# State space scan: in seven units of the last chunk GpSimd multiplies the states with C instead of VectorE

## The reference

```python
proj = jnp.einsum('blh,oh->bol', x, W_in); h, gate = jnp.split(proj, 2, axis=1)
h = silu(causal_depthwise_conv(h, conv_w) + conv_b)           # I = 512 channels, 4 taps
ts, Bm, Cm = jnp.split(jnp.einsum('bil,oi->blo', h, Wx), [R, R + N], axis=-1)   # R = 128, N = 16
ts, Bm, Cm = rms(ts), rms(Bm), rms(Cm)
delta = softplus(jnp.einsum('blr,ir->bil', ts, Wdt) + dt_bias)
def step(s, inp):                                             # s: [batch, I, N], over 256 steps
    s = jnp.exp(d_t[..., None] * A) * s + d_t[..., None] * B_t[:, None, :] * u_t[..., None]
    y = jnp.einsum('bin,bn->bi', s, C_t)
y = (ys + D * h) * silu(gate);  out = y @ Wout.T
```

## Time and profile before

| | us |
|---|---|
| median of 3 runs | 1913.19 (1912.94 to 1915.3) |
| the profiled execution's own time | 1918.9 |
| its span, first to last instruction | 1917.0 |
| TensorE busy in the span | 1812.9 (95%) |
| VectorE busy | 1339.2 (70%) |
| ScalarE busy | 943.0 (49%) |
| GpSimd busy | 576.9 (30%) |

### The profile page before, as it was taken

The page is one execution under the profiler, slowest core; times in us unless marked ns, Lnnn a source line. Parts: engine busy times, 40 slices in busy tenths (PEclk is TensorE's granted clock), DMA queues, the critical chain, the costliest instruction groups (busy, mean ns, idle before and its releaser), DMA issues.

```text
span 1917.0 us, 26237 instructions
## 1 busy us (share of the span) xinstructions
PE 1812.9 (95%) x9417; PEld 1378.8 (72%) x9417; DVE 1339.2 (70%) x1876; ACT 943.0 (49%) x1778; POOL 576.9 (30%) x397
## 2 busy tenths in 40 slices
PE   7999999999799999987789999999999999999998
PEld 5888888887354544433357888888888887777887
DVE  6666656567999999999975666565675555666533
ACT  4442333333688687684434433233333338888422
POOL 1000234000488878888710000000000025555000
PEclk9999999999899999999999999999999998999999
DMA  5232345120222222223102323231121306553100
GB/s 195 84 97 72 97 146 135 61 63 21 67 72 72 70 68 77 72 72 112 61 17 51 91 96 106 61 108 61 61 77 46 64 1 137 109 108 74 38 12 23
DMA packets 84187, 146.40 MB, mean 76 GB/s; under 512 B 13849, under 2 KB 23705, under 8 KB 83545
## 3 DMA queue, kind: packets, MB, share of 16 engines
q1 hardware_dynamic: 84056, 144.72, 26.5%
HBM read 130.38 MB, written 14.29 MB: 75 GB/s over the span
## 4 chain that ended last, share of the span: by engine, by line
PE 70%; DVE 16%; issue 6%; ACT 6%; DMA 1%; POOL 0%; DVEq 0%; SPq 0%; ACTq 0%; POOLq 0%
PE psum L161 19%; PE psum L162 18%; PE psum L163 18%; DVE scan_state L1608 8%; PE psum L1434 4%; PE psum L1982 2%; PE psum L1358 1%; PE psum L1329 1%; ACT psum L1542 1%; DVE moe_hidden_lo L850 1%; DVE scan_state L1615 1%; ACT L1485 1%; DVE X L807 1%; PE psum L1961 1%; ACT attn_p L2124 1%
## 5 line engine op out<-in xcount | busy, mean ns | idle before, releaser
L1207 POOL TENSOR_TENSOR scan_state<-scan_delta_u,scan_B_rows 128x1024 f32<-128x1024 f32 x127 | 299.5, 2367 | 99.9 <-PE psum L1434 85.7
L161 PE MATMUL psum<-xnT_hi,moe_w_hi 128*128 128x512 f32 x800 | 316.8, 396 | 6.3 <-DVE xnT_lo L470 6.3
L162 PE MATMUL psum<-xnT_lo,moe_w_hi 128*128 128x512 f32 x800 | 314.8, 393 | 0.0
L163 PE MATMUL psum<-xnT_hi,moe_w_lo 128*128 128x512 f32 x800 | 312.6, 391 | 0.0
L778 ACT ACTIVATE moe_hidden<-psum 128x512 f32<-128x512 f32 x200 | 119.6, 598 | 385.4 <-PE psum L163 385.3
L1608 DVE TENSOR_TENSOR_SCAN scan_state<-psum,scan_state 128x1024 f32<-128x1024 f32 x128 | 292.0, 2282 | 0.5 <-ACT psum L1542 0.4
L827 DVE TENSOR_TENSOR moe_gated_up<-moe_gate_rows,psum 128x512 f32<-128x512 f32 x184 | 126.4, 687 | 210.9 <-PE psum L163 121.3
L1434 PE MATMUL psum<-scan_state,ident 128*128 128x512 f32 x512 | 246.7, 605 | 4.6 <-DVE scan_gated L1623 3.4
L418 POOL TENSOR_SCALAR rstd<-mean_var 128x2 f32<-128x2 f32 x48 | 10.6, 220 | 763.5 <-DVE mean_var L452 763.1
L161 PE MATMUL psum<-moe_w_hi,moe_hidden_hi 128*128 128x256 f32 x800 | 230.3, 288 | 4.7 <-DVE moe_hidden_lo L850 3.6
L1542 ACT ACTIVATE psum<-scan_delta,scan_A 128x510 f32<-128x510 f32 x256 | 165.7, 679 | 126.8 <-DVE scan_state L1608 124.3
(11 more groups left out here) (225 smaller groups left out, 3479.7 us busy)
## 6 DMA issues: line engine op xcount, KB each, us to landing
scan_B_rows<-scan_B SPq DMA_DIRECT2D x127, 256.0 KB, 3.1
moe_gate_rows<-gate_table SPq DMA_DIRECT2D x176, 128.0 KB, 3.0
moe_w_raw<-moe_pack SPq DMA_DIRECT2D x50, 384.0 KB, 3.9
attn_stack<-attn_rows SPq DMA_DIRECT2D x96, 128.0 KB, 5.2
moe_gate_rows<-gate_table SPq DMA_DIRECT2D x32, 224.0 KB, 3.1
ffn_w_raw<-ffn_pack SPq DMA_DIRECT2D x16, 384.0 KB, 4.0
moe_gate_rows<-gate_table SPq DMA_DIRECT2D x32, 160.0 KB, 2.7
moe_gate_rows<-gate_table SPq DMA_DIRECT2D x24, 192.0 KB, 2.9
```

What stands on the lines that cost most here:

```text
L161: e.matmul(out, wH, xH, start=start, stop=False)
L162: e.matmul(out, wH, xL, start=False, stop=False)
L163: return e.matmul(out, wL, xH, start=False, stop=stop)
L1207: e.tensor_tensor(self.st[q % self.NBUF][:], self.dtu[:, 2 * h:2 * h + 2, :], self.Bs[:, q % self.RING, :].unsqueeze(1).broadcast_to([P, 2 ...
```

## The change

Seven units of the last chunk (`POOLED`: 2, 13, 17, 20, 23, 26, 29 within the chunk) are handled in another way. VectorE skips their product with C and TensorE skips the spread of their C row. SyncE instead spreads the C row with a DMA into a new buffer `Cs` in SBUF (one buffer, so each waits for the GpSimd product before it); this DMA is issued ahead of the B row of unit q+2. The table in HBM therefore holds 32 rows (B and C) and not 16, in all chunks. GpSimd multiplies the state buffer with that row, in its step q behind `inputs(q+3)`. TensorE takes the sum of such a unit one step later: in step q+1, after the wait for VectorE's product of unit q+1 and the spread, it waits for GpSimd's product and adds unit q, then unit q+1. The counts of the semaphores `z` and `C` are taken over the units that VectorE multiplies (`weighed`).

```diff
@@ -1018,6 +1018,7 @@
     NBUF = 4
     LAST = {12: ("ln0", 1 - NCH), 18: ("ln1", 1 - NCH)}
     RING = 4
+    POOLED = (2, 13, 17, 20, 23, 26, 29)
     BOTH = "natural_log_exp_and_others"
     BANK = 7
     ENDS = (7, 4)
@@ -1048,6 +1049,7 @@
         self.s_delta, self.s_dtu, self.s_Du = Sem(k, "delta"), Sem(k, "dtu"), Sem(k, "Du")
         self.s_dA, self.s_m, self.s_scan = Sem(k, "dA"), Sem(k, "m"), Sem(k, "scan")
         self.s_C, self.s_z, self.s_y, self.s_yg = Sem(k, "C"), Sem(k, "z"), Sem(k, "y"), Sem(k, "yg")
+        self.s_crow, self.s_zp = Sem(k, "crow"), Sem(k, "zp")
         self.s_o, self.s_tap, self.s_b0 = Sem(k, "o"), Sem(k, "tap"), Sem(k, "b0")
         tail.by_act, tail.s_pw = 2, Sem(k, "pw", 4, passes=NCH)
 
@@ -1086,6 +1088,7 @@
         self.mean = [new("mean_ts", [P, P]), new("mean_bc", [2 * NST, 2 * NST])]
         self.eps = new("eps", [P, 1])
         self.dtb, self.A, self.D = new("dt_bias", [P, IB]), new("A", [P, IB, NST]), new("D", [P, IB])
+        self.Cs = new("C_row", [P, CHUNK])
         self.eye, self.pick = new("state_pick_raw", [P, 2 * NST]), new("state_pick", [P, 2 * NST], F32R)
         assert a.off <= k.nc.sbuf_usable_end, a.off
         acc = Arena(k, tag)
@@ -1108,6 +1111,17 @@
 
         c, r = divmod(q, 2 * NST)
         return c, r // NST, r % NST
+
+    def pooled(self, q):
+
+
+        c, r = divmod(q, self.UNITS)
+        return c == NCH - 1 and r in self.POOLED
+
+    def weighed(self, q):
+
+        n = sum(self.pooled(x) for x in range(q + 1))
+        return q + 1 - n, n
 
     def job(self, q):
 
@@ -1147,15 +1161,25 @@
                           (self.mean[1], "mean_bc")):
             e.dma_start(dst[:], i[name]).then_inc(self.s_load.sem, 16)
 
+    def c_row(self, e, q):
+
+        used = self.weighed(q)[1] - 1
+        if used:
+            e.wait_ge(self.s_zp.sem, self.s_zp.at(used))
+        c, h, n = self.unit(q)
+        e.dma_start(self.Cs[:], self.table[c, NST + n].partition_broadcast(P)).then_inc(self.s_crow.sem, 16)
+
     def sync(self, e):
         for q in range(self.N):
             c, h, n = self.unit(q)
+            if q >= 2 and self.pooled(q - 2):
+                self.c_row(e, q - 2)
             if q == self.N - self.UNITS + 12 and self.next:
                 self.emptied(e)
                 self.next.first(e)
             if q % self.UNITS == 0:
                 e.wait_ge(self.s_nm.sem, self.s_nm.at(2 * c + 2))
-                e.dma_start(self.table[c], self.wt[1][0:NST, :]).then_inc(self.s_kept.sem, 16)
+                e.dma_start(self.table[c], self.wt[1][:]).then_inc(self.s_kept.sem, 16)
                 e.wait_ge(self.s_kept.sem, self.s_kept.at(16 * (c + 1)))
             if q > self.RING:
                 e.wait_ge(self.s_m.sem, self.s_m.at(q - self.RING + 1))
@@ -1208,6 +1232,13 @@
                             self.Bs[:, q % self.RING, :].unsqueeze(1).broadcast_to([P, 2, CHUNK]),
                             ALU.mult).then_inc(self.s_m.sem, 1)
 
+        def weigh(q):
+            st, n = self.st[q % self.NBUF], self.weighed(q)[1]
+            e.wait_ge(self.s_scan.sem, self.s_scan.at(q + 1))
+            e.wait_ge(self.s_crow.sem, self.s_crow.at(16 * n))
+            e.tensor_tensor(st[:], st[:], self.Cs[:].unsqueeze(1).broadcast_to([P, 2, CHUNK]),
+                            ALU.mult).then_inc(self.s_zp.sem, 1)
+
         for slot in (0, 2):
             self.before.pool(e, NCH - 1, slot)
         for q in range(1, 3):
@@ -1220,6 +1251,8 @@
                 self.normed(e, c + 1, 1)
             if q + 3 < self.N:
                 inputs(q + 3)
+            if self.pooled(q):
+                weigh(q)
             if r in (6, 8, 9, 11):
                 (self.lose, self.lost, self.step, self.times_u)[(6, 8, 9, 11).index(r)](e, c, 1)
             if r in (24, 25, 26, 28) and c + 1 < NCH:
@@ -1411,6 +1444,8 @@
             e.wait_ge(self.s_relu.sem, self.s_relu.at(2))
 
         def spread(q):
+            if self.pooled(q):
+                return
             c, h, n = self.unit(q)
             if q and q % self.UNITS == 0:
                 e.wait_ge(self.s_bc.sem, self.s_bc.at(c + 1))
@@ -1418,21 +1453,29 @@
             e.matmul(ps[:, 6, :], self.pick[:, x:x + 1].broadcast_to([P, P]), self.bc[:, c % 2, :], start=True,
                      stop=True).then_inc(self.s_C.sem, 1)
 
+        def total(q):
+            n = q % NST
+            for m in range(2):
+                x = e.matmul(ps[:, 4 + m, :], k.ident[:], self.st[q % self.NBUF][:, m, :], start=(n == 0), stop=(n == NST - 1))
+            x.then_inc(self.s_y.sem, 1)
+
         begin()
         spread(0)
         for q in range(self.N):
             c, h, n = self.unit(q)
             if n == 0 and q:
-                e.wait_ge(self.s_z.sem, self.s_z.at(q + 1))
+                e.wait_ge(self.s_z.sem, self.s_z.at(self.weighed(q)[0]))
                 spread(q + 1)
                 e.wait_ge(self.s_yg.sem, self.s_yg.at(2 * c + h))
             if n or not q:
-                e.wait_ge(self.s_z.sem, self.s_z.at(q + 1))
+                e.wait_ge(self.s_z.sem, self.s_z.at(self.weighed(q)[0]))
                 if q + 1 < self.N:
                     spread(q + 1)
-            for m in range(2):
-                x = e.matmul(ps[:, 4 + m, :], k.ident[:], self.st[q % self.NBUF][:, m, :], start=(n == 0), stop=(n == NST - 1))
-            x.then_inc(self.s_y.sem, 1)
+            if q and self.pooled(q - 1):
+                e.wait_ge(self.s_zp.sem, self.s_zp.at(self.weighed(q)[1]))
+                total(q - 1)
+            if not self.pooled(q):
+                total(q)
             if self.job(q):
                 job(self.job(q), self.BANK)
             for m in self.DIAG.get(q % self.UNITS, ()):
@@ -1609,9 +1652,11 @@
                                  ALU.add).then_inc(self.s_scan.sem, 1)
 
         def weigh(q):
+            if self.pooled(q):
+                return
             st = self.st[q % self.NBUF]
             e.wait_ge(self.s_scan.sem, self.s_scan.at(q + 1))
-            e.wait_ge(self.s_C.sem, self.s_C.at(q + 1))
+            e.wait_ge(self.s_C.sem, self.s_C.at(self.weighed(q)[0]))
             e.tensor_tensor(st[:], st[:], ps[:, 6, :].unsqueeze(1).broadcast_to([P, 2, CHUNK]), ALU.mult).then_inc(self.s_z.sem, 1)
 
         def gate(c, h):
@@ -2405,7 +2450,7 @@
         tails = [Tail(k, "t0_", entry=True, route=True)]
         pack = nc.dram_tensor("ffn_pack", [FFN_TILES, P, Glu.WCOLS], F32, kind="Internal").ap()
         gates = nc.dram_tensor("gate_table", [NEXP, TOK], F32, kind="Internal").ap()
-        states = nc.dram_tensor("scan_B", [NCH, NST, CHUNK], F32, kind="Internal").ap()
+        states = nc.dram_tensor("scan_rows", [NCH, 2 * NST, CHUNK], F32, kind="Internal").ap()
         rows = nc.dram_tensor("attn_rows", [2, 2, NCH, HID, CHUNK], F32, kind="Internal").ap()
         fixed = nc.dram_tensor("attn_fixed", [2, 64, CHUNK], F32, kind="Internal").ap()
         parts = []
```

## The result

The change made the kernel slower: 1925.37 us median of 4 runs (1922.42 to 1928.03) against 1914.14 (1912.94 to 1915.3), ratio 1.0056 [1.0043, 1.0068]. Five more runs gave 1926.96 against 1914.39, ratio 1.006 [1.0048, 1.0072]. The forecast was 1915.9 in a range up to 1920.5: the side was right, the size was not.

The account below looks back on a forecast made before the run. VectorE was taken to bound the last chunk before the change, GpSimd's loop after it. 2.4 us saved and 5.1 us lost to TensorE's half clock gave +2.7, so 1915.9 us, range 1908.5 to 1920.5.

Parts of the forecast that it names:

- The bound and the gross saving: VectorE sets the last chunk's pace; seven multiplies leaving it save 1.27 us each, 8.9 us in all.
- Unit 2: At TensorE's output job: it starts 1.71 us earlier and scan 5 moves from 872.30 to 870.6, saving 1.7 us.
- Unit 13: GpSimd's multiply comes only after input 16 ends at 907.3; of 3.0 us saved so far, 1.5 is left.
- The loop: Units 17 to 29: GpSimd's multiply, wait for TensorE's sum and three inputs take 11.4 us; 2.4 us saved overall.
- TensorE's clock: Bursts of sums after TensorE's waits: three of five run at half clock, 1.71 us each, costing 5.1 us.
- every burst slow: Rival: TensorE's bursts all at half clock; five give +6.2 us, 1919.4, six give 1921.1; chance 0.18.
- The sum again: The forecast's total for the change: -2.4 + 5.1 = +2.7 us.
- the step that carried the change over: Profiled execution 1918.9 becomes 1921.6; the shown median, 1913.19, is 5.7 below it, so the forecast is 1915.9 us.
- Rows by DMA, table, skipped spreads: Seven C rows, the 32-row table and seven spreads left out on TensorE: taken as 0 us.
- The row of unit 22: B row queued behind C row 20 after multiply 17: lands at 928.9, wanted at 929.4, hidden by 0.5 us.

Follow-up runs that it names:

- e3: The change, with matmuls that add 0 to the open sums filling TensorE's waits: 1916.01 us, 1.0015 to the kernel before.
- e10: The change's program with the 32-row table and no units given to GpSimd: ratio 1.0001 to the kernel before.
- e4: The change, with GpSimd's multiply of unit q put ahead of the input of unit q+3: 1915.08 us, 1.0001 to the kernel before.
- e11: The change with only units 2, 17, 21, 25, 29 given to GpSimd, order as in the change: ratio 1.0037 to the kernel before.
- e12: The change with only units 17, 20, 23, 26 given to GpSimd: 1920.6 us, 1.0034 to the kernel before.
- e1: Only the change's 32-row table and seven C row DMAs, which nobody reads; VectorE and TensorE do all units: ratio 1.0009 to the kernel before.
- e9: The change itself run again, nothing altered: 1926.96 us, 1.006 to the kernel before.
- e8: The change's program with no units given to GpSimd and matmuls adding 0 behind units 5, 12, 21, 23, 26, 28: 1.0015 to the kernel before.
- e2: The change with only unit 2 given to GpSimd: ratio 0.9998 to the kernel before.
- e6: The change with only units 2 and 26 given to GpSimd: ratio 0.9987 to the kernel before.

## Why the prediction was wrong

- **The bound and the gross saving** were right. VectorE's multiplies left, and two scans in a row take 4.46 (2.19 forecast from start to start).
- **Unit 2**: 1.5 us gained up to scan 5 (1.7 forecast). Right.
- **Unit 13**: GpSimd's multiply at 906.85, 56.1 after scan 0; forecast 907.3, that is 56.0 after it. Right, but the burst behind it was already slow: scan 17 lies 67.4 after scan 0, where 65.2 was forecast and before had 66.7.
- **The loop**: right in kind and in length (11.4 forecast, 11.5 in e3). Its result, 2.4 us saved, was too good: e3 shows 0 against before's stretch with one slow burst of 1.0 us, so some 1 us saved, and against e10's stretch a loss of 1.4. The sum had started from the execution with both long weight splits (2.23 and 3.02) and called them part of the loop; where one is short anyway (e10) there is 2.1 less to save. The order experiment (e4) shows that it was a matter of order and not of GpSimd's load.
- **TensorE's clock**: this step failed, by its size. The prediction took 3 of 5 bursts from the share among five waits of before, 5.1 us. Six of six were slow. GpSimd's waits are 1.85 longer four times and 1.0 once, and the last burst 1.7: 10.1 us. The granted clock's level and the price of a slow sum were right; the share was wrong. It was counted over the length of waits, and length alone does not tell: the last burst was slow behind 1.49 and 0.93 us, and behind the same wait for the gate of unit 16 a sum was slow in e11 (first line) and not in e12 (second):

```profile
918.63 3.21 PE L1459 MATMUL psum<-scan_state,ident 128*128 128x512 f32 x4 [2.47 <-DVE scan_gated L1668]
917.77 1.96 PE L1459 MATMUL psum<-scan_state,ident 128*128 128x512 f32 x4 [2.46 <-DVE scan_gated L1668]
```

  That waits close together are what made all six slow is my reading and not shown. The rival "every burst slow" (six: 1921.1) was the nearest. The Trainium skill (TensorE: Matmul & The Clock Gate, Part 1: The HAM clock gate) has the array slow until activity releases it. This trace agrees for the four bursts that began at the low level, and not for the two that began at full clock and fell 1 us in.
- **The sum again**: with these terms -1 + 10.1 = +9 for the stretch, against 8.7 measured from before's; +1.4 + 10.1 = +11.5 against 11.0 measured from e10's. The first, carried to the median, is 1923, 2 to 4 us short of the runs; the second is 1925.6, and the runs gave 1925.4 and 1927.0. So the step that carried the change over from an execution 5.7 us above the median hid some 2 us.
- **Rows by DMA, table, skipped spreads**: 0 was right (e1, e10). The row of unit 22, forecast as hidden by 0.5 us, released no wait: all of GpSimd's waits from 905 on end with TensorE's sums.
- **What was in it only once**: TensorE's in-order wait holds back the C rows for VectorE (2.95 at unit 16; 6.2 in e11). For unit 16 the prediction had 1.0.

## What to carry to other kernels

Work given to an idle engine pays only if its result is wanted late: here the spare 41 us did not help, because each product stood behind an input that nobody needed yet and in front of one that waited for it; with the two exchanged (e4) 10 us came back. Put the product that closes a loop first in the queue, and the one with slack behind it. When a change makes TensorE wait and then work in bursts, price its bursts at half clock unless something keeps it busy; matmuls that add zero gave back 8 to 11 us here. And before a sum starts from one profiled execution, look at what it has beside its median, and at a second execution: here two executions of the same work differed by 2.3 us inside the stretch.

## What the hardware showed that I had not expected

Two slow stretches of TensorE's clock, at the start of the scan stage (from 493 or 496 to 507 or 510 us of the span) and at the last chunk's first gate (its sum takes 3.4 to 3.7 us, not 1.9), stand at the same place of the work in all sixteen profiled executions, and the six slow bursts of the change came back one by one in e9. That they follow from the work in front, and not from chance, is the likely reading. The sum behind the second gate fits it: behind the same waits it took 1.98 us in before, e1, e8 and e10 and 3.0 in e2 and e6, where unit 2 is GpSimd's and no other ahead of it. Other slow stretches come and go: the one near 49 us is in six of the sixteen, whose last chunk begins at 852.7 to 853.6 and not at 850.8 to 851.4, and in the attention stage there are 3.4, 6.8 or 10.2 us at half clock.

A weight split on VectorE took 0.95 us when no instruction of GpSimd was under way as it began. Where one was, the split ended 0.8 us after that one and took 1.1 to 3.1 (3.02 in before, 1.88 with the change). Scans in the same position kept their 2.28.

And a filler matmul takes 0.23 us and keeps the clock at the level of 2.4 GHz: 0.98 granted from 905 on in e3, against 0.79.
